# Routed rows of a mixture-of-experts layer: written out and summed at the end, or added to the residual in memory by a chain of adding scatters

## The reference, cut to what matters

```
h   = layernorm(x1) * (1 + cb) + sb
shared = (silu(h @ sh_gate.T) * (h @ sh_up.T)) @ sh_down.T           # inner width 512
probs  = softmax(h @ wg.T)                                           # 8 experts
top_w, top_idx = top_k(probs, 2);  top_w = top_w / sum(top_w)
routed = sum over the token's two experts e of
         top_w[e] * (silu(h @ gate[e].T) * (h @ up[e].T)) @ down[e].T
out = x1 + gb * (shared + routed)                                    # gb: one row of 256 for each batch
```

## Time and profile before

| | us |
|---|---|
| median of 3 runs (442.6 to 445.05) | 443.52 |
| the profiled execution's own time | 444.21 |
| its span, first to last instruction | 442.1 |
| PE busy in the span | 401.8 (91%) |
| DVE busy | 310.1 (70%) |
| ACT busy | 261.8 (59%) |
| POOL busy | 187.3 (42%) |
| mean DMA rate | 94 GB/s |

### The profile page before, as it was taken

The page is one execution under the profiler, slowest core; times in us unless marked ns, Lnnn a source line. Parts: engine busy times, 40 slices in busy tenths (PEclk is TensorE's granted clock), DMA queues, the critical chain, the costliest instruction groups (busy, mean ns, idle before and its releaser), DMA issues.

```text
span 442.1 us, 11571 instructions
## 1 busy us (share of the span) xinstructions
PE 401.8 (91%) x4075; PEld 289.9 (66%) x4100; DVE 310.1 (70%) x626; ACT 261.8 (59%) x495; POOL 187.3 (42%) x194
## 2 busy tenths in 40 slices
PE   7999997999989898975999999999999999999971
PEld 3555455788767788965656555666666666679970
DVE  5986576889699733899556777768577655544597
ACT  4488663766676457371577666586766656566320
POOL 6000022477757742003114888865555554522100
PEclk9799996999999999997999999999999999999997
DMA  8860020000850169911001111111211111110592
GB/s 271 285 76 15 0 97 0 3 14 26 311 168 15 38 225 299 323 74 37 25 25 49 37 58 53 60 61 49 73 49 62 61 61 61 50 37 25 169 341 87
DMA packets 23566, 41.67 MB, mean 94 GB/s; under 512 B 3108, under 2 KB 16404, under 8 KB 23384
## 3 DMA queue, kind: packets, MB, share of 16 engines
q1 hardware_dynamic: 16888, 28.44, 19.9%
q0 software_dynamic: 3744, 10.23, 7.2%
q10 hardware_dynamic: 2880, 2.26, 1.5%
HBM read 31.23 MB, written 9.69 MB: 93 GB/s over the span
## 4 chain that ended last, share of the span: by engine, by line
PE 50%; DVE 25%; issue 11%; ACT 8%; DMA 3%; ACTq 1%; DVEq 1%; SPq 0%
PE ps L1360 18%; PE ps L1392 10%; PE ps L1368 6%; PE ps L1205 4%; DVE wx L840 4%; PE ps L1377 3%; DVE tmp L1061 2%; DVE tmp L1055 2%; PE ps L1337 2%; PE ps L1199 2%; DMA wx<-in_wexp 2%; DVE wx L1096 1%; DVE xres L901 1%; DVE tmp L915 1%; DVE st L904 1%
## 5 line engine op out<-in xcount | busy, mean ns | idle before, releaser
L1360 PE MATMUL ps<-wx,tmp 128*128 x448 | 104.9, 379 | 2.8 <-issue 1.2
L481 POOL DMA_INDIRECT parts<-tmp,dst_i x39 | 57.5, 1475 | 68.7 <-DVE tmp L1076 68.1
L1392 PE MATMUL ps<-wx,tmp 128*128 (+1 forms) x660 | 81.1, 273 | 2.6 <-DVE h2s L1081 2.5
L682 ACT ACTIVATE tmp<-tmp 128x512 bf16<-128x512 f32 x55 | 34.7, 632 | 75.0 <-DVE tmp L1055 59.9
L1360 PEld LDWEIGHTS ps<-wx,tmp 128*128 128x128 bf16 x468 | 44.0, 98 | 49.7 <-issue 7.9
L1392 PEld LDWEIGHTS ps<-wx,tmp 128*128 128x128 bf16 x660 | 63.6, 98 | 19.2 <-DVE tmp L1061 2.5
L476 POOL DMA_INDIRECT tmp<-h2rows,src_i x39 | 39.1, 1003 | 58.0 <-DVE src_i L1017 31.8
L1055 DVE TENSOR_TENSOR tmp<-ps,tmp 128x512 f32<-128x512 f32 x55 | 37.8, 687 | 35.7 <-PE ps L1360 17.0
L1368 PE MATMUL ps<-tmp,wx 128*128 128x128 bf16 x768 | 48.4, 225 | 1.4 <-ACT tmp L675 1.4
L1067 DVE SCALAR_TENSOR_TENSOR woutg<-modr,w_hl,woutg 128x256 f32<-128x256 f32 x39 | 18.9, 486 | 42.9 <-ACT woutg L691 38.5
L1368 PEld LDWEIGHTS ps<-tmp,wx 128*128 128x128 bf16 x768 | 46.2, 101 | 1.6 <-issue 1.5
(11 more groups left out here) (184 smaller groups left out, 692.2 us busy)
## 6 DMA issues: line engine op xcount, KB each, us to landing
wx<-in_wexp SPq DMA_DIRECT2D x27, 512.0 KB, 5.2
wx<-parts SPq DMA_DIRECT2D x16, 256.0 KB, 6.4
xres<-in_x SPq DMA_DIRECT2D x4, 512.0 KB, 7.2
h2rows<-h2s ACTq DMA_DIRECT2D x16, 128.0 KB, 3.1
out<-wx SPq DMA_DIRECT2D x16, 128.0 KB, 2.9
h2s<-in_wmod SPq DMA_DIRECT2D x1, 1024.0 KB, 11.2
wx<-decay_rows SPq DMA_DIRECT2D x16, 64.0 KB
modr<-mod_rows SPq DMA_DIRECT2D x1, 1024.0 KB, 4.6
```

Of the source, the lines that this page charges most:

```text
L481: e.indirect_dma_start(t["parts"], bass.IndirectOffsetOnAxis(ap=dst_i[:, j:j + 1], axis=0), yb[(NA + j) % 2], None).then_inc(s_left[(NA + ...
L682: e.activation(hs[p][:, 0:FF], hf[p], ACT.Copy).then_inc(s["inner_high"], 1)
L1360: ins = e.matmul(ps[:, bank, :], xT[p][:, (2 * a + k) * P:(2 * a + k + 1) * P], wx[:, bass.ds(at_ + weights(part, w) + k * FF, FF)], start ...
L1392: ins = e.matmul(half(DOWN_BANKS[p], 0, D), inner[:, (KF * a + k) * P:(KF * a + k + 1) * P], wx[:, bass.ds(off, D)] if routed(f) else wx[: ...
```

## The change

- The result rows are no longer written to places of their own. x1 is stored to a memory tensor `sums` (2048 rows, and 128 for empty rows) by seven SP transfers, and each routed tile's rows are added to it by an indirect DMA that adds (`compute_op=ALU.add`). As two tiles can hold the same token, `add_rows(j)` waits until the adding scatter before it has landed (`rows_added`, 16 * j). One row of a token occurs once in a tile.
- The weights w1 and w2 are stored to a memory tensor by SP as soon as they are made, and POOL gathers them by slot, 128 values of 4 bytes for each routed tile (`gather_weights`), through four semaphores. `make_inner` of a routed tile multiplies them in: a scalar_tensor_tensor with a scalar for each partition in place of a tensor_tensor.
- The exp moves from step 10 to step 5 in ACT's list, followed by a silu of one column. `behind` moves to the front of routing, w1 and w2 into step 6, and a few small operations for the indices are added.
- `base` on POOL keeps its product and loses its addition. At the end each token tile is read once (128 KB), and DVE makes one tensor_tensor, gb * shared + sum, in the order that SUMS_AT gives.

```diff
-        ROUTING_AT = {4: 18, 5: 2, 6: 2, 7: 13, 8: 3, 11: 3}
-        RANK_AT, MARK_AT, FIND_AT, EXP_AT = 4, 5, 7, 10
+        ROUTING_AT = {4: 19, 5: 2, 6: 5, 7: 15, 8: 4}
+        RANK_AT, MARK_AT, FIND_AT, EXP_AT = 4, 5, 7, 5
-        PARTS_AT = {NF - 4: range(0, 1), NF - 3: range(1, 4), NF - 2: range(4, 7), NF - 1: range(7, 10), NF: range(10, 13),
-                    NF + 1: range(13, NT)}
-        LAST_AT = {NF: range(NA, 10), NF + 1: range(10, 13), NF + 2: range(13, NT - 1)}
+        SUMS_AT = {NF - 3: (9, 10, 0), NF - 2: (11, 1, 2, 3), NF - 1: (12, 4, 5, 6), NF: (13, 7, 8), NF + 1: (14,), NF + 2: (15,)}
+        SUM_ORDER = [g for f in SUMS_AT for g in SUMS_AT[f]]
...
@@ SP: after load_expert(1, 2)
+            def store_x1(first, last):
+                e.wait_ge(s["x1_made"], last)
+                for b in range(B):
+                    tiles_ = slice(first // B + NC * b, last // B + NC * b)
+                    e.dma_start(t["sums"][0:B * S, :].rearrange("(t p) d -> p t d", p=P)[:, tiles_, :], xres[:, tiles_, :]).then_inc(s["x1_stored"], 16)
+            store_x1(0, 8)
+            e.dma_start(t["sums"][B * S:B * S + P, :], xres[:, 0, :]).then_inc(s["x1_stored"], 16)
+            store_x1(8, 12)
...
@@ SP: after the last load_expert
+            store_x1(12, NT)
+            e.wait_ge(s["routing"], RT_WEIGHTS)
+            e.dma_start(t["weights"].rearrange("(p m) a -> p (m a)", p=P), w12).then_inc(s["weights_stored"], 16)
-            for i in range(2):
-                e.wait_ge(s_left[(NA + i) % 2], 16 * ((NG + 1 - i) // 2))
+            e.wait_ge(s["rows_added"], 16 * NG)
             e.wait_ge(s["down_product"], NA + NG)
-            for g in range(NT):
+            for g in SUM_ORDER:
                 tile = tile_of(g)[0]
-                e.dma_start(parts_in[:, tile], t["parts"][0:NPART, :].rearrange("(a t p) d -> p a t d", a=TOP, p=P)[:, :, tile, :]).then_inc(s_parts[g], 16)
+                e.dma_start(summed_in[:, tile], t["sums"][0:B * S, :].rearrange("(t p) d -> p t d", p=P)[:, tile, :]).then_inc(s_sum[g], 16)
...
@@ POOL
-            def scatter(j):
+            def gather_weights(j):
+                e.indirect_dma_start(slot_w[:, j:j + 1], None, t["weights"],
+                                     bass.IndirectOffsetOnAxis(ap=weight_i[:, j:j + 1], axis=0)).then_inc(s_w[j % 4], 16)
+            def add_rows(j):
                 wait(e, "result_made", j + 1)
-                e.indirect_dma_start(t["parts"], bass.IndirectOffsetOnAxis(ap=dst_i[:, j:j + 1], axis=0),
-                                     yb[(NA + j) % 2], None).then_inc(s_left[(NA + j) % 2], 16)
+                wait(e, "rows_added", 16 * j)
+                e.indirect_dma_start(t["sums"], bass.IndirectOffsetOnAxis(ap=dst_i[:, j:j + 1], axis=0),
+                                     yb[(NA + j) % 2], None, compute_op=ALU.add).then_inc(s["rows_added"], 16)
...
             gather(0)
             gather(1)
+            e.wait_ge(s["rows_found"], 2)
+            e.wait_ge(s["weights_stored"], 16)
+            gather_weights(0)
             for j in range(NG + 4):
                 if j + 2 < NG:
                     gather(j + 2)
+                if j + 1 < NG:
+                    gather_weights(j + 1)
+                if j == 4:
+                    e.wait_ge(s["rows_found"], 3)
+                    e.wait_ge(s["x1_stored"], 16 * (3 * B + 1))
                 if 0 <= j - 4:
-                    scatter(j - 4)
+                    add_rows(j - 4)
                 if 0 <= j - 6 < NA:
                     base(j - 6)
...
@@ DVE: make_inner, take_result, and the end
-                    e.tensor_tensor(hf[p], ps[:, UP_BANKS[p], :], sg[p], ALU.mult).then_inc(s["inner_made"], 1)
+                    if routed(f):
+                        j = f - NA
+                        wait(e, s_w[j % 4], 16 * (j // 4 + 1))
+                        e.scalar_tensor_tensor(out=hf[p], in0=ps[:, UP_BANKS[p], :], scalar=slot_w[:, j:j + 1], in1=sg[p],
+                                               op0=ALU.mult, op1=ALU.mult).then_inc(s["inner_made"], 1)
...
-                    wait(e, s_left[f % 2], 16 * (j // 2))
+                    wait(e, "rows_added", 16 * (j - 1))
...
+            def add_up(g):
+                tile = tile_of(g)[0]
+                e.wait_ge(s_sum[g], 16)
+                if g < NA:
+                    wait(e, "base_weighted", g + 1)
+                else:
+                    wait(e, "last_weighted", g - NA + 1)
+                e.tensor_tensor(summed_in[:, tile], shared_out[:, tile], summed_in[:, tile], ALU.add).then_inc(s["summed"], 1)
```

More of the change, by code:

```diff
@@ L191, in build @@
         sel = route(TOP * NT * NE).rearrange("p (c t e) -> p c t e", c=TOP, t=NT)
-        mx, f1, mx2, f2, behind, e2, den, w1, w2 = (route(NT) for _ in range(9))
+        mx, f1, mx2, f2, behind, e2, den = (route(NT) for _ in range(7))
+        w12 = route(TOP * NT)
+        w1, w2 = w12[:, 0:NT], w12[:, NT:TOP * NT]
         picked = route(NT * NE // 2).bitcast(bf16)
@@ L198, in build @@
         late_i = route(NG, i32)
+        of_slots = dk[:].rearrange("p h d -> p (h d)")
+        weight_f, slot_w = of_slots[:, 0:NG], of_slots[:, NG:2 * NG]
+        place_i, none_i, weight_i, dst_i = (of_slots[:, i * NG:(i + 1) * NG].bitcast(u32) for i in range(2, 6))
         tiles, tiles_end, base = (route(NE) for _ in range(3))
@@ L968, in routing @@
                 assert count[0] == RT_PICKED
+                yield link(e.tensor_tensor(behind, mx2, mx, ALU.subtract))
+                assert count[0] == RT_BEHIND
                 e.wait_ge(s["ranks"], 1)
@@ L1007, in routing @@
                                           ALU.is_equal).then_inc(s["low_marked"], 1)
+                e.wait_ge(s["routing_exp"], 1)
+                yield link(e.tensor_scalar(den, e2, 1.0, None, ALU.add))
+                yield link(e.reciprocal(w1, den))
+                yield link(e.tensor_tensor(w2, e2, w1, ALU.mult))
+                assert count[0] == RT_WEIGHTS
                 e.wait_ge(s["ranks"], 2)
@@ L1032, in routing @@
                 assert count[0] == RT_SLOTS
-                yield link(e.tensor_tensor(behind, mx2, mx, ALU.subtract))
-                assert count[0] == RT_BEHIND
+                yield link(e.tensor_scalar(none_i, place_i, TOP * B * S, 1, ALU.bitwise_and, ALU.logical_shift_right))
+                e.wait_ge(s["rows_found"], 2)
+                yield e.tensor_tensor(dst_i, none_i, src_i[:], ALU.add).then_inc(s["rows_found"], 1)
                 e.tensor_scalar(late_i, src_i[:], S, None, ALU.is_ge)
@@ L1038, in routing @@
                 assert count[0] == RT_FLAGS
-                e.wait_ge(s["routing_exp"], 1)
-                yield link(e.tensor_scalar(den, e2, 1.0, None, ALU.add))
-                yield link(e.reciprocal(w1, den))
-                yield link(e.tensor_tensor(w2, e2, w1, ALU.mult))
             def take_rows(f):
```

72 lines of the change are left out of this document (26 added, 46 removed).

## The result

| | before | after |
|---|---|---|
| median, us | 443.88 (442.6 to 445.05, 4 runs) | 453.45 (451.92 to 455.87, 4 runs) |
| span of the profiled execution | 442.1 | 453.9 |

The change is slower: after is 1.0221 times before, with a 95% interval of 1.0167 to 1.0276, some 9.6 us. The prediction was 438.1 us, with 451 as the upper end of its range. The profiled execution of after took 455.87 us, the longest of its four.

The account below looks back on a forecast made before the run. PE was to bound the routed tiles from 300 us and DVE the end. On the 442.1 us span, 0.9 - 2.2 + 0.6 + 2.3 - 7.0 = -5.4 led to 438.1 us at the median, range 432.5 to 451.

Parts of the forecast that it names:

- Routing, +0.9: DVE's chain ahead of the first gather: four more small operations, all on the path, +0.9 us (0.7 to 1.5).
- The exp, -2.2: ACT's list: table loads and exp leave step 10 for an idle wait at step 5, -2.2 us.
- The inner product, 757 ns: DVE's routed inner product with the weight: 757 ns instead of 687, counting in nine steps, +0.6 us (0 to +2.7).
- POOL's queue, +2.3: POOL's turns with weight gather and adding scatter: 4.35 to 4.56 us of a 4.59 step, +2.3 us (0 to +20).
- 4.4 us of slack: Result buffers: POOL may fall back 4.4 us if adds land 1.0 later, so the nine base turns just fit.
- link of the chain: Successive adding scatters on POOL: 1.65 + 2.2 + 0.3 = 4.15 us a link, under the 4.59 us step, not binding.
- The end, -7.0: Behind 416 us: DVE's 16 additions replace about 17 us of work with about 6, -7.0 us (-8.0 to -4.0).
- SP's path: The end: last add landed at 417.3, then 16 reads and 16 stores at 0.51 us, landed at 435.8.
- SP's first read: Start of the end on SP: a first read later than 419 us was to show the prediction wrong.
- B: POOL's list, turns 6 to 36, becomes the bound through costlier adds or weight gathers: 446 us (443 to 453), chance 0.17.
- C: Chain of add landings binds, a link taking 5.1 us (2.9 behind generation): about 455 us, chance 0.12.
- E: Steps of 5.12 us: DVE's and POOL's colliding work miss each other, 4.5 us less, 433.5 us, chance 0.09.

Follow-up runs that it names:

- e4: Kernel before with the routing part alone: exp moved to step 5, small operations added; 441.57 us, 0.9965 of before.
- e11: Changed kernel with the two waits ahead of each adding scatter swapped, weight gathers kept; 445.93 us, 1.0045 of before.
- e12: Changed kernel with weights by TensorE products instead of small gathers, the two waits in the changed kernel's order; 438.85 us, 0.9924 of before.
- e10: Changed kernel with weights by TensorE products instead of small gathers, and the two waits of an add swapped; 438.27 us, 0.9867 of before.
- e1: Changed kernel without the 39 weight gathers, a constant 0.5 as every slot's weight; 438.38 us, 0.9926 of before.
- e9: Changed kernel without weight gathers (constant 0.5) and with the two waits of an add swapped; 437.28 us, 0.9852 of before.
- e8: Changed kernel without weight gathers (constant 0.5) and with overwriting scatters instead of adds, chain kept; 434.1 us, 0.984 of before.
- e13: Changed kernel with weight gathers kept, overwriting scatters instead of adds, and the two waits swapped; 434.09 us, 0.9838 of before.
- e2: Changed kernel with overwriting scatters instead of adds, weight gathers, chain and order of waits kept; 446.7 us, 1.0039 of before.
- e3: Kernel before plus 39 unused gathers of 4 bytes a partition, which nobody waits for; 463.28 us, 1.0454 of before.
- e5: Changed kernel with each add going to rows of its own, so adds don't wait for each other; 440.56 us, 0.9966 of before.
- e6: Changed kernel with 19 weight gathers issued before the first add, none in the base turns, 20 from turn 15; 443.7 us, 1.0015 of before.
- e7: Kernel before plus 39 unused gathers of 64 bytes a partition, each waiting for the fourth before it to land; 450.13 us, 1.0182 of before.

## Why the prediction was wrong

1. *Routing, +0.9.* The first gather starts at 205.75 instead of 203.02, +2.7, but in the nine profiles with the same routing it starts between 202.07 and 205.75, on average at 204.0: about +1. Right within what single profiles can tell.
2. *The exp, -2.2.* From the first gather to the first result it is 28.75 us instead of 31.73 (28.6 to 28.8 in the nine profiles), so this part gave about 2.9. The two together measure -1.5 us alone (e4) where -1.3 was predicted: right in sum.
3. *The inner product, 757 ns.* 747. Right; 0.6 us is not visible beside the rest.
4. *POOL's queue, +2.3.* **This step failed.** Its durations held: the add 1.63 to 1.7 us to generate (1.65 taken), 2.2 behind that to land for the last adds (2.2 taken), the weight gather 0.974 (0.97 taken). Three things made of them were wrong:
   - The fall-back was to be absorbed by 4.4 us of slack, counted from the scatter to the buffer of results. But the gathers of rows stand in the same queue behind the scatter, and PE waits for them; the chain above hands every turn's 0.8 us on at once (5.91 against 5.12). The turn was priced 0.5 over, with the row gather at 0.97 where five of those in the base turns take 1.80 us. By tile 12 this is +4.4 us. The Trainium skill's lock of the shared port pair, cited in the prediction (SBUF - State Buffer, section SBUF: two separate sides), is the likely mechanism, and I had applied it to the scatter and not to the gather in the sum. The trace agrees with it in part: in each of the five, DVE's L877, L1080 and L1100 all run beside the gather. But other gathers of after take 0.99 beside 0.83 to 0.97 us of L877 without the other two (at 303.66, 308.29 and 313.06) or beside the other two without L877 (363.51 and 368.09), and before has scatters of 0.99 wholly beside a weight half (at 239.37, 298.02 and 334.88), so that "1.72 where it meets DVE's weight halves" was read too simply. What makes the difference was not tested.
   - The link of the chain was 1.65 + 2.2 + 0.3 = 4.15; the 0.3 is a wake-up that holds when the DMA instruction itself carries the landing wait (0.26 in e11). As the change orders its waits it is 0.73, and a link 4.5 to 4.6 with nothing left of a step of 4.57. Together with the lag of the last add it cost 0.6 to 0.7% (e12 to e10, e1 to e9).
   - The late results of TensorE had no place in the sum at all. They make the jumps from tile 17 on, up to 9.3 us of the 15.2; swapping the two waits takes back 7.4 behind tile 12 (e11). Why they come stays open.
5. *The end, -7.0.* -9.1 behind the last landing, 19.5 us where the reckoning of SP's path gives 18.5 (435.8 - 417.3). Its path for PE was never put to the test, since the landing came 17 us later than the 417.3 reckoned, nearly all of it from step 4. That is also the one sign of being wrong that was met: SP's first read at 434.37, where later than 419 was to be wrong. A slip without effect: 426.49 + 0.7 + 0.4 + 1.5 is 429.1 and not 428.8.

Of the rivals, B named the right place, POOL's list, and a time of 446; C named the chain with a link of 5.1 and 455. Parts of both happened, and neither was the mechanism as told: POOL's queue binds through the row gathers behind the scatter and not through a slower add, and the chain through the wake-up and not the landing. E, the collisions that go, is seen in the profile of e1 (55.9 us up to tile 12 against 59.2 in e9), not in after. The signs given for B (POOL over 95% busy) were not met either, though POOL was the bound in the base turns, since "issue" time between its DMAs isn't counted as busy. The other steps stand: without step 4 the prediction comes to 435.8 us, and e8, which has neither the small gathers nor the adds, gives 0.984 of 443.52, 436.4.

## What to carry to other kernels

When instructions are added to a queue, count the slack from the queue's nearest customer, not from the instruction that was lengthened: here the gathers behind the scatter were it. A wait that sets a chain's rate should be carried by its DMA instruction and not by one of its own; in these kernels that meant to write it *first* of the two waits, and the trace's instruction records tell which of them the DMA carries. Here a swap of two lines was worth 0.6 to 2%. Beside adding scatters, a small table lookup by an indirect DMA in every turn cost 1.8% more (e10 to e11) than 32 small products and six DVE operations once; beside plain scatters it cost nothing that could be measured (e13).

## What the runs showed of the hardware that was not expected

In these traces an adding indirect DMA is cut into smaller packets. The queue of indirect DMAs from 300 to 370 us, before and then after (packets, MB, share of 16 engines):

```profile
q0 software_dynamic: 1449, 3.93, 17.4%
```

```profile
q0 software_dynamic: 3203, 3.77, 33.6%
```

The trace has a plain scatter of 128 rows as 32 packets of 4096 bytes (median 180 ns in this stretch, with those of the row gathers) and an adding one as 128 packets of 1024 bytes (median 102 ns). The engines are busy about twice as long for the same rows; the small gathers don't explain it, since e2 has them beside plain scatters at 16.9%. A landing comes 3.6 to 5.6 us after the start (median 3.9, e11) where an overwriting one comes after 2.2 to 2.9 (e13). With 0.34 of the engines' time this was not a bound.

The late results of TensorE stay without a cause. What the runs show: signals of products that PE's records have as finished arrive together, several within 1 us, after 2 to 5 us; the profiles of the changed kernel, e2 and e3 have them, all with gathers of 4 bytes a partition. No profile without such gathers has them, but nor have those of e5, e6, e11 and e13, which have the same gathers. In e11 and e13 the DMA instruction itself carries the landing wait, and in e5 POOL waits for no landing; yet e3 has no chain either and shows them (20 us of "remote" waits), and e6 has the old order and doesn't. So small gathers are needed as far as seen, and the instruction of its own that waits makes them likelier, without being the cause. Each kernel was profiled once, and one profile can miss them: the runs of e6 reach from 439.21 to 450.39 us and those of e2 from 440.76 to 452.15, as if they came in some runs and not in others. But the medians over all runs (e2 against e13, the changed kernel against e11) move in the same way. Gathers of 4 bytes with a wait, or of 64 bytes without one, would separate the two differences of e7; neither was run. Whether TensorE stood still or only its signals were held can't be told, since the ends of matmuls in these records are modelled.
